# AdaLN and a top-2 mixture of experts on one core: another order of weights, loads and Gram groups, and first scales by GpSimd

## What is computed

```python
ys = cond * 256 ** -0.5
d = rsqrt(einsum('bi,io->bo', ys * ys, W * W) + 1e-8)
y = einsum('bsi,io->bso', x * ys[:, None, :], W) * d[:, None, :]
lang = softmax(y @ lang_w.T + lang_b)                        # 4 languages
ew = pad(lang)[..., idx] + pad(lang)[..., idx + 1]           # idx = arange(8) % 4
p, i = top_k(softmax(y @ router_w.T + router_b + 0.1 * ew), 2)
p = p / p.sum(-1, keepdims=True)
h = gelu(einsum('bsd,edh->bseh', y, w1) + b1, approximate=False)   # 8 experts, 256 -> 1024
o = einsum('bseh,ehd->bsed', h, w2) + b2                           # 1024 -> 256
return x + (p[..., None] * take_along_axis(o, i[..., None], 2)).sum(2)
```

## Time and profile before

| | us |
|---|---|
| median of 3 runs | 323.06 (322.9 to 324.74) |
| the profiled execution | 323.72 |
| its span, first to last instruction | 321.9 |
| PE busy, of the span | 281.6 |
| DVE, ACT, POOL busy | 201.4, 195.9, 164.9 |

### The profile page before, as it was taken

The page is one execution under the profiler, slowest core; times in us unless marked ns, Lnnn a source line. Parts: engine busy times, 40 slices in busy tenths (PEclk is TensorE's granted clock), DMA queues, the critical chain, the costliest instruction groups (busy, mean ns, idle before and its releaser), DMA issues.

```text
span 321.9 us, 9020 instructions
## 1 busy us (share of the span) xinstructions
PE 281.6 (87%) x3103; PEld 234.6 (73%) x3103; DVE 201.4 (63%) x462; ACT 195.9 (61%) x419; POOL 164.9 (51%) x145
## 2 busy tenths in 40 slices
PE   8998829999975909999999999999999999999810
PEld 6866729888765908988888888888888878888500
DVE  2945887695658957556757666665756666575610
ACT  2545476496589293676675757676675757667500
POOL 8000104600767762657576675767676675745430
PEclk9999956999998976999999999999999999999975
DMA  6899991799155030322423233242323223231320
GB/s 169 320 402 320 364 324 32 236 385 379 16 182 166 5 63 2 52 52 35 66 39 51 52 43 61 35 68 36 60 44 50 53 39 66 34 51 18 35 20 13
DMA packets 24104, 35.72 MB, mean 111 GB/s; under 512 B 4144, under 2 KB 19968, under 8 KB 23904
## 3 DMA queue, kind: packets, MB, share of 16 engines
q1 hardware_dynamic: 14464, 24.69, 21.7%
q0 software_dynamic: 7488, 10.39, 19.9%
q10 hardware_dynamic: 2112, 0.08, 0.4%
HBM read 27.61 MB, written 9.64 MB: 116 GB/s over the span
## 4 chain that ended last, share of the span: by engine, by line
PE 49%; POOL 16%; issue 10%; DVE 9%; DMA 9%; ACT 2%; SPq 1%; POOLq 0%; DVEq 0%; ACTq 0%
PE ps L576 20%; PE ps L593 18%; POOL out L413 8%; POOL onehot L406 5%; PE ps L482 4%; DMA out<-onehot,idx 4%; DMA out<-in_x 4%; POOL rows L387 3%; DVE wsp L852 3%; DMA wsp<-in_x 2%; PE ps L496 2%; PE ps L568 2%; SPq L338 1%; PE ps L455 1%; PE ps L553 1%
## 5 line engine op out<-in xcount | busy, mean ns | idle before, releaser
L576 PE MATMUL ps<-onehot,wsp 128*128 128x128 f16 x1872 | 159.6, 221 | 7.4 <-DVE wsp L852 7.4
L576 PEld LDWEIGHTS ps<-onehot,wsp 128*128 (+1 forms) x1872 | 133.7, 97 | 39.5 <-DVE wsp L852 7.6
L736 ACT ACTIVATE pay<-ps,cur 128x128 f32<-128x128 f32 x312 | 117.3, 460 | 65.8 <-issue 49.6
L593 PE MATMUL ps<-wsp,pay 128*128 (+1 forms) x616 | 140.6, 318 | 1.2 <-DVE pay L1019 1.2
L413 POOL DMA_INDIRECT out<-onehot,idx x39 | 73.6, 1887 | 16.9 <-POOL onehot L406 9.2
L1019 DVE SCALAR_TENSOR_TENSOR pay<-pay,cur 128x512 f16<-128x512 f32 x72 | 54.7, 760 | 36.1 <-ACT pay L724 34.8
L406 POOL TENSOR_SCALAR onehot<-onehot,cur 128x256 f32<-128x256 f32 x37 | 36.8, 994 | 76.4 <-DVE onehot L1037 39.9
L387 POOL DMA_INDIRECT rows<-y_rows,idx x39 | 45.1, 1156 | 22.0 <-issue 11.6
L593 PEld LDWEIGHTS ps<-wsp,pay 128*128 128x128 f16 x616 | 49.4, 98 | 3.9 <-issue 1.6
L1013 DVE TENSOR_SCALAR pay<-pay,cur 128x512 f16<-128x512 f32 x36 | 19.8, 551 | 31.2 <-ACT pay L736 31.2
L695 ACT ACTIVATE wsp<-stage,wscale 128x2048 f16<-128x2048 f32 x10 | 19.8, 2002 | 13.6 <-DVE wscale L845 7.1
(11 more groups left out here) (170 smaller groups left out, 214.6 us busy)
## 6 DMA issues: line engine op xcount, KB each, us to landing
stage<-in_L_ffn_w SPq DMA_DIRECT2D x10, 1024.0 KB, 9.7
wsp<-in_L_ffn_w SPq DMA_DIRECT2D x6, 1024.0 KB, 12.4
y_rows<-pay SPq DMA_DIRECT2D x4, 512.0 KB, 7.2
wsp<-in_x SPq DMA_DIRECT2D x3, 512.0 KB, 8.1
b2bc<-in_L_ffn_b SPq DMA_DIRECT2D x1, 1024.0 KB, 5.5
rows<-y_rows,idx POOLq DMA_INDIRECT x39, 3.4
out<-onehot,idx POOLq DMA_INDIRECT x39, 4.0
wsp<-in_x SPq DMA_DIRECT2D x2, 256.0 KB, 5.7
```

Source lines behind the costliest of these rows:

```text
L576: last = mm(ps[:, HB + (2 * j + g) % RING, c * P:(c + 1) * P], wsp[:, bass.ds(e, 1), o:o + P].rearrange("p a f -> p (a f)"), xsp[:, j % RI ...
L593: last = mm(ps[:, OB + j % 2, 0:width], hsp[:, (2 * j + g) % NH, part, c, :], wsp[:, bass.ds(e, 1), o + w:o + w + width].rearrange("p a f ...
L736: last = a.activation(to, ps[:, HB + (2 * j + g) % RING, c * P:(c + 1) * P], ACT.Gelu, bias=cur[:, j % RING, cc:cc + 1], scale=cur[:, j % ...
```

## The change

- `PLACE`, `SPLIT_ORDER`, `GROUPS` and the order of SP's loads are others. Group 2 is now (1, 9), and the first scales (groups 0 to 2, `EARLY_GROUPS`) are made by POOL (`scale_early`) from sums that ACT copies out of PSUM (`copy_sums`); each group has its own semaphores and its own PSUM bank from a list.
- `HIGHS` and the new `LOWS` place high and low halves by half turn (2j + 1 and 2j + 2 of turn j); Gram groups 4 to 6 likewise.
- In the y phase the transpositions of x for pairs 6 and 7 and those for the maxima stand elsewhere, on PE and on DVE.
- There are five tables `cur`, and `expert_table(j)` waits for `o_ready` of j-5. DVE copies the transposed rows from tile 5 on (from 8 before).
- POOL waits for `x_copied` behind its first weighting. p's two writes to `y_rows` are issued by SP, not by ACT.

The diff, cut (index changes from `% RING` to `% CURS` and semaphores' names left out):

```diff
-PLACE = (0, 7, 1, 4, 2, 5, 3, 6, 8, 9, 0, 1, 2, 3, 0, 1)
-SPLIT_ORDER = (0, 2, 4, 6, 7, 8, 1, 9, 10, 11, 12, 13, 3, 5, 14, 15)
-SPLITS = {0: (6, 7), 1: (8, 1), 2: (9, 10), 3: (11, 12), 4: (13, 3), 5: (5, 14), 6: (15,)}
-HIGHS = {0: (8, 1), 1: (9, 10), 2: (11, 12), 3: (13, 3), 4: (5,), 5: (14, 15)}
-GROUPS = ((0, 2, 4), (6, 7), (8, 9), (1, 3, 5), (10, 11), (12, 13), (14, 15))
-GRAMS = {1: 4, 2: 5, 4: 6}
+PLACE = (0, 4, 3, 8, 2, 3, 7, 9, 6, 5, 2, 1, 0, 5, 1, 2)
+SPLIT_ORDER = (0, 2, 4, 6, 9, 8, 3, 7, 11, 1, 10, 12, 13, 14, 15, 5)
+HIGHS = {0: (0, 2, 4, 6, 9), 1: (8, 3), 2: (7,), 3: (11,), 5: (1, 10), 7: (12,), 9: (13,), 11: (14,), 13: (15,), 15: (5,)}
+LOWS = {1: (4,), 2: (6, 9, 8, 3), 3: (7,), 4: (11,), 5: (1, 10), 7: (12,), 9: (13,), 11: (14,), 13: (15,), 15: (5,)}
+GROUPS = ((0, 2, 4), (6, 8, 11), (1, 9), (3, 7), (10, 12), (5, 13), (14, 15))
+GRAM_BANKS = (7, 5, 6, 7, 5, 7, 5)
+EARLY_GROUPS = 3
+GRAMS = {4: 4, 7: 5, 9: 6}
+XACT = 5
+CURS = 5
...
-            for n in (0, 2, 4, 6, 1, 7):
+            for n in (0, 4, 2, 11, 8, 6):
                 load_weights(n)
...
                     sp.wait_ge(x_max, len(XCHUNKS) - 1)
-                    load_weights(3)
-            for n in (8, 9, 5):
-                load_weights(n)
+                    load_weights(1)
+                if c == 1:
+                    load_weights(9)
+            load_weights(3)
+            sp.wait_ge(p_ready, 1)
+            for b in range(NB):
+                sp.dma_start(y_tiles[:, b, :, D:ROW], payv[:, b * TB:(b + 1) * TB, D:ROW]).then_inc(p_written, 16)
+            load_weights(7)
             for j in range(RING):
                 sp.wait_ge(gathered[j], 16)
+            load_weights(12)
             sp.dma_start(b2bc[:, :, :].rearrange("p e d -> p (e d)"),
                          b2.rearrange("(a e) d -> a (e d)", a=1).broadcast_to([P, E * D])).then_inc(b2_in, 16)
-            for n in (10, 11, 12, 13):
-                load_weights(n)
+            load_weights(10)
+            load_weights(5)
             for b in range(NB):
                 sp.dma_start(out[b * SEQ:(b + 1) * SEQ, :], x[b]).then_inc(x_copied, 16)
+            load_weights(13)
             for n in (14, 15):
                 load_weights(n)
...
             g.tensor_tensor(pex, lg[:, :, 0:E], over(s1[:, 3, :], E), ALU.subtract).then_inc(p_in, 1)
+            def scale_early(g_):
+                pool.wait_ge(w_raw, g_ + 1)
+                g.tensor_scalar(of_group(wround, g_), of_group(wraw, g_).bitcast(I32), 2.0 ** -24, ROUND, ALU.mult,
+                                ALU.add).then_inc(w_rounded, 1)
+                pool.wait_ge(w_rounded, g_ + 1)
+                g.tensor_scalar(of_group(wscale, g_).bitcast(I32), of_group(wround, g_), -ULP,
+                                (FIELD_SCALE + 1 + ROUND) * ULP, ALU.mult, ALU.add).then_inc(w_scaled[g_], 1)
+                for n in GROUPS[g_]:
+                    c = column(n)
+                    last = g.tensor_scalar(wt[:, n:n + 1], wround[:, c:c + 1], -(ROUND + 1), 1.0, ALU.add, ALU.mult)
+                last.then_inc(w_t[g_], 1)
+            scale_early(0)
             pool.wait_ge(second, 1)
             g.tensor_tensor(pe1[:, 0, :], s1[:, 4, :], s1[:, 3, :], ALU.subtract).then_inc(p_in, 1)
...
+            scale_early(1)
+            scale_early(2)
...
-                if j == 0:
-                    pool.wait_ge(x_copied, 16 * NB)
                 if j < NT - 2:
                     pool.wait_ge(o_read, j + 1)
...
+                if j == 0:
+                    pool.wait_ge(x_copied, 16 * NB)
+                else:
                     pool.wait_ge(added, 16 * j)
...
             for t in range(T):
                 rows_of_y(t)
-                if t in (1, 3, 5, 7):
-                    transpose_x(4 + t // 2)
-                if t == 2:
+                if t == 1:
+                    tr(ps[:, SB, BM:BM + E * KF], b1r[:, :], ...)
+                    transpose_x(4)
+                if t == 3:
+                    transpose_x(5)
                     pe.wait_ge(ym_ready, 1)
                     tr(ps[0:1, SB, YMAX:YMAX + P], ysm[:, :], ident[:, :]).then_inc(ym_psum, 1)
-                if t == 3:
+                if t == 4:
                     pe.wait_ge(y_max, 1)
                     mm(ps[:, SB, YS:YS + 1], ones32[0:1, :], ymax[0:1, 1:2], start=True, stop=True).then_inc(ys_psum, 1)
+                    transpose_x(6)
+                    transpose_x(7)
+                    tr(ps[0:E, SB, 256:256 + P], bmx[:, :], ident[:, :]).then_inc(bm_psum, 1)
...
             gram(0)
             gram(1)
             sum_squares(0)
-            sum_squares(1)
...
             last.then_inc(ranked, 1)
+            sum_squares(1)
+            gram(2)
+            sum_squares(2)
             pe.wait_ge(tok_hot, 1)
...
             last.then_inc(mapped, 1)
-            gram(2)
             gram(3)
...
             gram_sums(0)
-            gram_sums(1)
+            copy_sums(0)
             act.wait_ge(p_in, 2)
             a.activation(pex, pex, ACT.Exp).then_inc(p_exp, 1)
             a.activation(pe1[:, 1, :], pe1[:, 0, :], ACT.Exp).then_inc(p_exp, 1)
+            gram_sums(1)
             a.activation(warm[:, :], pe1[:, 0, 0:1], ACT.Gelu)
-            act.wait_ge(p_ready, 1)
-            for b in range(NB):
-                act.dma_start(y_tiles[:, b, :, D:ROW], payv[:, b * TB:(b + 1) * TB, D:ROW]).then_inc(p_written, 16)
-            for n in SPLIT_ORDER[0:5]:
-                split_high(n)
+            split_high(0)
+            copy_sums(1)
+            gram_sums(2)
+            split_high(2)
+            copy_sums(2)
+            split_high(4)
+            split_high(6)
+            split_high(9)
...
             gelu_table(0, 3)
+            gram_max(3)
             split_low(0)
-            gram_max(2)
             expert_table(0)
-            scale_weights(2)
             split_low(2)
-            gram_max(3)
             expert_table(1)
-            split_low(4)
             scale_weights(3)
...
-                if j >= RING:
-                    dve.wait_ge(o_ready, j - RING + 1)
+                if j >= CURS:
+                    dve.wait_ge(o_ready, j - CURS + 1)
```

More of the change, by code:

```diff
@@ L264, in wait_split, with column @@
             eng.wait_ge(w_split, SPLIT_ORDER.index(n) + 1)
-        def gram_bank(g):
-            return 5 if g % 2 else 7
         def group_of(n):
             return [n in halves for halves in GROUPS].index(True)
+        def column(n):
+            return [m for halves in GROUPS for m in halves].index(n)
         def of_group(ap, g):
[L273 to L276, removed]
+            n = column(GROUPS[g][0])
+            return ap[:, n:n + len(GROUPS[g])]
         def experts_of(engine, j, n):
@@ L486, in gram @@
             def gram(g):
-                if g >= 2:
-                    pe.wait_ge(w_scaled, g - 1)
-                if g == 1:
+                for h in range(g):
+                    if GRAM_BANKS[h] == GRAM_BANKS[g]:
+                        if h < EARLY_GROUPS:
+                            pe.wait_ge(w_raw, h + 1)
+                        else:
+                            pe.wait_ge(w_scaled[h], 1)
+                if GRAM_BANKS[g] == SB:
                     pe.wait_ge(nfb_ready, 1)
@@ L495, in gram @@
                         cols = half[:, c * P:(c + 1) * P, 1]
-                        last = mm(ps[:, gram_bank(g), i * P:(i + 1) * P], cols, cols, start=(c == 0),
+                        last = mm(ps[:, GRAM_BANKS[g], i * P:(i + 1) * P], cols, cols, start=(c == 0),
                                   stop=(c == HALF // P - 1))
-                last.then_inc(gram_done, 1)
+                last.then_inc(gram_done[g], 1)
             def sum_squares(g):
-                if g < 2:
-                    pe.wait_ge(w_sq, (3, 5)[g])
-                else:
-                    pe.wait_ge(w_max, g - 1)
-                mm(ps[:, gram_bank(g), WS:WS + len(GROUPS[g])], ones32[:, :], of_group(wsum, g), start=True,
-                   stop=True).then_inc(w_psum, 1)
+                if g < EARLY_GROUPS:
+                    pe.wait_ge(w_sq, sum(len(h) for h in GROUPS[0:g + 1]))
+                else:
+                    pe.wait_ge(w_max, g - EARLY_GROUPS + 1)
+                mm(ps[:, GRAM_BANKS[g], WS:WS + len(GROUPS[g])], ones32[:, :], of_group(wsum, g), start=True,
+                   stop=True).then_inc(w_psum[g], 1)
             pe.wait_ge(consts, 11)
@@ L602, in blocks @@
                         wait_split(pe, 2 * j)
+                    if j == E:
+                        pe.wait_ge(w_split, 1 + max(SPLIT_ORDER.index(n) for n in range(0, 2 * E, 2)))
                     if g == 0:
@@ L607, in blocks @@
                     if j < DIRECT:
-                        pe.wait_ge(w_in[PLACE[2 * j + 1]], 16)
+                        pe.wait_ge(w_in[PLACE[2 * j + 1]], 16 * (len(earlier(2 * j + 1)) + 1))
                         pe.wait_ge(gelu_done, 2 * j + g + 1)
@@ L614, in blocks @@
```

(18 more changed lines are left out.)

133 lines of the change are left out of this document (72 added, 61 removed).

## The result

The changed kernel takes 303.32 us (median of 4 runs, 302.16 to 303.86) against 322.98 of the kernel before on the same chip: a ratio of 0.937, 95% interval 0.934 to 0.940, so -19.7 us. The forecast was -13.7 and 309.4, and 303.3 lies just under its range of 304 to 317. The direction, the places and the mechanism of the stalls were right; one term of the sum was too large by more than its bound. A run more than 1.5% above the fastest of its kernel counts as a slow one: of the medians further down, that of the kernel with three tables holds two such runs and that of the one with weight 5 ahead holds one; without them they are 305.78 and 315.64.

What follows compares the result with a forecast made beforehand. PE's own work bounds the kernel, with 17.6 us of waits and low clock before turn 8 to win. First block -2.1, turns 0 to 7 -11.6 (-17.6 + 6): -13.7, so 309.4 us, range 304 to 317.

Steps and rivals of the forecast that it cites:

- Part (4): Turns 0 to 7: stalls gone, -17.6 us, including PE's waits of 7.4 (weight 14), 3.4 (load 15), 1.8 (rows).
- Part (5): Turns 0 to 7: slips, 4.0 ScalarE and VectorE, 1.0 before GELU 2, 1.0 GpSimd; bounds 2 and 12 us.
- Term A: Start of the first up block, at 59.57 us before: -2.1 us, bounds +1 and -4.
- Part (1): y phase: transpositions regrouped, Gram groups begin at 32.3 instead of 33.37; -1.1 us, bounds -1.5 and +1.
- Part (2): Routing: first scales by GpSimd, VectorE's reciprocal at about 41.55, 41.39 before; -0.7 us left, bounds +1 and -1.5.
- Part (3): Ahead of the first block: group 2 goes into PE's wait, PE ready 3.9 us earlier; rows 1 there at about 57.2.
- Part (6): p's two writes on SP's queue behind 1 MB loads, load 7 behind them, covered by the routing: costed at nothing.
- 1: Rival: VectorE and ScalarE pace the turns, turns 1 to 7 at 7.2 us, slips 12, time 315.4; chance 0.25.
- 2: Rival: GpSimd becomes the bound, its work falling behind low halves, 10.4 us a turn, time 332; chance 0.06.
- 4: Rival: another late weight or load stops PE, clock halves again, 11 of 17.6 us come back, 320.4; chance 0.06.
- 3: Rival: p's writes wait behind the loads, all gathers start some 5 us late, time 314.5; chance 0.08.

Runs made afterwards that it cites:

- three tables: The changed kernel with three tables instead of five, so turn j's table waits for the weighting of turn j-3: 307.60 us, ratio 0.951.
- weight 5 ahead: The changed kernel with the split of weight 5 moved ahead of those of weights 14 and 15: 316.79 us, ratio 0.979.
- group 2 late: The changed kernel with Gram group 2 and its sum behind the mapping of slots instead of ahead of it: 311.53 us, ratio 0.963.
- three extra instructions: The changed kernel with three extra VectorE instructions, outputs unused, in each of turns 3 to 7: 307.31 us, ratio 0.948.
- both undone: The changed kernel with three tables instead of five and GpSimd's wait for the copy of x ahead of its first weighting: 307.42 us, ratio 0.949.
- control: The changed kernel itself run again, nothing changed: 303.18 us, ratio 0.938.
- low half 0 first: The changed kernel with VectorE's maximum of Gram group 3 behind the low half of weight 0, not ahead of it: 304.08 us, ratio 0.939.
- three warming products: The changed kernel with the maximum of Gram group 3 behind weight 0's low half and three warming products instead of six: 305.41 us, ratio 0.942.
- one extra instruction: The changed kernel with one extra VectorE instruction, output unused, in each of turns 3 to 7: 302.82 us, ratio 0.937.
- wait ahead of weighting: The changed kernel with GpSimd's wait for the copy of x back ahead of its first weighting, five tables kept: 304.51 us, ratio 0.942.

## Why the prediction was right or wrong

**What bounds it, right.** The 17.6 us of idle and slow PE between the first block and turn 8 were the thing to win, and PE's own work there was taken as 57.1 us; measured it is 56.6. Steady stage and tail did not change, as said.

**Part (4), right in all three.** The 7.4, 3.4 and 1.8 us and both low stretches of the clock are gone. The order was named as the cause of the 7.4, and putting weight 5 back ahead brings 6.4 back. The order of loads, named for the 3.4, was not tested by itself. The decoupling was given a role in the 1.8 us and, through VectorE's slip, in the later ones; on its own it wins 1.8 of the 15.4 us between turns 3 and 8.

**Part (5), the step that failed.** It added 6.0 us of new slips, with a lower bound of 2, and the stretch shows -0.5: 6.5 of the 7.0 us by which the sum missed the span. Three mistakes are in it. The sums of 5.7 and 5.8 us a turn were compared with PE's 5.59 and the small difference was made into 0.8 by adding "waits for PE". But a wait for PE on the other engine is the sign that PE is the slower one; it costs nothing. Measured, VectorE is busy 4.87, 5.40 and 5.61 us and ScalarE 5.36, 5.51 and 5.51 in turns 5 to 7, so neither is over. Second, the lead: Gram groups lengthen PE's turns 1, 3 and 4 to 8.7, 8.2 and 7.6 us, in which VectorE does its extra 1 to 2 us. Third, the four low halves in a row were computed to leave a margin of some 3.5 us for table 2 (it came at 71.66 us, forecast 72), and 1.0 us was added all the same; GpSimd's 1.0 had no term behind it either. A computed margin was overruled by a feeling three times, always to the same side. The bound 2 should have been 0: nothing in the rows excluded that all slips fit.

**Term A, right in kind, small by 0.7.** Forecast -2.1, measured -2.8, of which the matmul on the counts is 1.3 us earlier, the way from it to the index 0.9 shorter, and the rest 0.6. Part (1) said that the Gram groups would begin at 32.3; they began at 32.11. Part (2) expected VectorE's reciprocal at 41.55 and a nearly spent gain. It came at 40.39, since GpSimd could round the sums from 38.25 on. The timelines of POOL and DVE in the changed kernel:

```profile
38.25 0.30 POOL L395 TENSOR_SCALAR wround<-wraw 128x3 f32<-128x3 int32 x1 [1.53 <-ACT wraw L721]
...
40.39 0.25 DVE L972 RECIPROCAL pe<-pe 128x16 f32<-128x16 f32 x1 [0.18 <-POOL pe L409]
```

VectorE waited 0.18 us for GpSimd, not 1.25. Part (3) was right that group 2 fits into the wait ahead of the mapping. It did not name that GpSimd's scales of that group gate the gathers, which the run with group 2 late showed, and it was wrong on what comes last ahead of the first block. It named rows 1. In the changed kernel it is PE's own stream (PE's timeline):

```profile
51.27 1.89 PE L529 MATMUL ps<-wsp 128*128 128x128 bf16 x16 [1.00 <-DMA wsp<-in_L_ffn_w]
52.96 2.76 PE L593 MATMUL ps<-onehot,ones 128*128 128x512 f16 x6
55.51 0.48 PE L603 MATMUL ps<-ident,rows 128*128 128x128 f32 x2
56.56 0.41 PE L603 MATMUL ps<-ident,rows 128*128 128x128 f32 x2 [0.56 <-ACT onehot L772]
```

The second half of Gram group 3 waits 1.00 us for the load of weight 7, the warming products behind it run at the lower clock (2.76 us; the same six took 1.46 in the kernel before), and the transpositions follow without a wait for rows.

**Part (6), right for the gathers, not for load 7.** The first gather (timeline of POOL, changed kernel) ends its idle time on VectorE's index, not on a transfer:

```profile
50.32 1.18 POOL L416 DMA_INDIRECT rows<-y_rows,idx  x1 [1.85 <-DVE idx L1013]
```

But part (6) put load 7, behind p's writes, at nothing too, and that is the load that PE waited 1.00 us for. The two writes hold SP's queue for 2.35 us, and the load is issued only at 43.55. Six profiled executions have the same instructions up to there and the early start of the last section. In three of them the writes hold the queue for 1.99 to 2.27 us, PE waits 0.28 to 0.42 for the load, and the first block comes at 55.6 to 55.7; in the other three it is 2.35, 3.00 and 3.46 us, with waits of 1.00, 1.34 and 2.98 and the block at 56.81, 57.43 and 58.27. No run moved the load, so what an earlier one would win is an estimate from these, about 1 us.

**The rivals.** 1, 2 and 4 did not come. Of 1 the run with three extra instructions shows how near it was: under 4.3 us of work over five turns. For 2, GpSimd was held up beside low halves, but in the first turns, where it had 13.9 us to spare. The timelines of POOL and of DVE in the changed kernel there:

```profile
74.58 2.95 POOL L433 TENSOR_SCALAR onehot<-onehot,cur 128x256 f32<-128x256 f32 x1 [13.92 <-DVE onehot L1083]
78.69 3.55 POOL L442 DMA_INDIRECT out<-onehot,idx  x1 [1.16 <-DVE cur L1059]
```

```profile
74.39 2.34 DVE L910 SCALAR_TENSOR_TENSOR wsp<-stage,wscale,wsp 128x2048 f16<-128x2048 f32 x1
...
78.36 2.34 DVE L910 SCALAR_TENSOR_TENSOR wsp<-wsp,wscale 128x2048 f16<-128x2048 f32 x1
```

The low half ends at 76.73 and the weighting at 77.53, 0.80 later, about the 0.92 that it takes alone; the scatter ends 1.54 behind its low half. The Trainium skill (SBUF — State Buffer, "Who interferes with whom") says that a GpSimd instruction that reads SBUF contends with a VectorE one that has two SBUF inputs, and that the second to start blocks until the first has ended. The trace agrees with it twice. 3 did not come either: the first gather's line above shows it. Of 4's sign, a Gram group that waits for a load, only the 1.00 us ahead of the first block came. Taking the sum without part (5), -19.7 us, gives the -19.7 of the medians; that fit is part luck, as the span fell by 20.7, A was 0.7 short, and a wait that nobody forecast (load 7) is in it.

## What to carry over

When an engine off the path has its work for a stage added up and it comes out just under or at the period of the engine on the path, write down zero and its margin, not a surcharge; then measure the margin with a dummy instruction, which takes one run. In an order that several engines share as a count ("so many splits done"), an item that nobody needs yet delays every item behind it, and what forces it forward is often the buffer that it sits in: change the place first. A stall of TensorE can cost more than its length: two waits, 9.2 us in all, became 12.8, because the clock was at 0.50 behind each. It need not: with both undone, waits of 0.99 and 2.22 us in turn 3 left the clock at 1.00.

## What the runs showed of the hardware

The start of an execution comes out in several ways, with the same instructions. In the changed kernel and its control the clock was at 1.2 GHz for some 3.4 us about the tenth. In the runs with both undone, with three extra instructions, with low half 0 first and with three warming products it stayed there until about 18 us, and VectorE's reciprocal, that all share, came at 43.05 to 43.30 us and not at 40.4. The windows (columns as in the earlier trace rows) from 8 to 18 us show it, first in the changed kernel:

```profile
8.00:18.00 10.00, 9.37 (x51) 8.06 (x52) 8.27 (x19) 3.87 (x6) 0.89 (x1) 0.83 0.85 336
```

Then in the kernel with three extra instructions:

```profile
8.00:18.00 10.00, 8.88 (x32) 7.52 (x32) 7.90 (x16) 2.71 (x5) 0.84 (x1) 0.50 0.89 329
```

The edit of the second lies 70 us later. What tips the clock one way or the other stays open.

These 2.7 us do not all arrive. With both undone and with three extra instructions the first up block is at 57.67 and 57.63 us. Where the reciprocal came at 40.4 to 40.7, the block lies anywhere from 55.63 (one extra instruction) to 58.27 (wait ahead of weighting), and there it goes with PE's wait for the load of weight 7. The two ends of that range, from PE's timelines, first one extra instruction, then the wait ahead of weighting:

```profile
50.96 1.89 PE L530 MATMUL ps<-wsp 128*128 128x128 bf16 x16 [0.36 <-DMA wsp<-in_L_ffn_w]
```

```profile
53.56 1.89 PE L529 MATMUL ps<-wsp 128*128 128x128 bf16 x16 [2.98 <-DMA wsp<-in_L_ffn_w]
```

So the first block moves by 2.6 us between executions, more than most of the single edits here are worth, and a single profile is best compared from one anchor to another behind it.
